# Attention: three of a key tile's four maximum products placed behind the value products

## What is computed

```python
# x: (2, 2048, 256); H = 256, NH = 16 heads, D = 16
hn = _layernorm(x, ln1_g, ln1_b)
q = (hn @ wq + bq).reshape(b, s, NH, D).transpose(0, 2, 1, 3)
k = (hn @ wk + bk).reshape(b, s, NH, D).transpose(0, 2, 1, 3)
v = (hn @ wv + bv).reshape(b, s, NH, D).transpose(0, 2, 1, 3)
scores = jnp.einsum('bhqd,bhkd->bhqk', q, k) / jnp.sqrt(jnp.float32(D))
attn = jax.nn.softmax(scores, axis=-1)
o = jnp.einsum('bhqk,bhkd->bhqd', attn, v)
```

## Time and profile before

| | |
|---|---|
| median of 3 runs | 3656.47 us (3653.67 to 3663.54) |
| the profiled execution | 3660.14 us, its span 3658.3 us |
| attention, first S to last exponential | 1521.1 to 2948 us of the span |
| VectorE's reductions (line 694) | 2048, 1269.9 us busy |
| TensorE's X, S, V | 2048, 2048 and 4096 matmul records |

### The profile page before, as it was taken

The page is one execution under the profiler, slowest core; times in us unless marked ns, Lnnn a source line. Parts: engine busy times, 40 slices in busy tenths (PEclk is TensorE's granted clock), DMA queues, the critical chain, the costliest instruction groups (busy, mean ns, idle before and its releaser), DMA issues. The chain is left out here.

```text
span 3658.3 us, 43277 instructions
## 1 busy us (share of the span) xinstructions
PE 3051.2 (83%) x12860; PEld 1452.0 (40%) x12860; DVE 2599.6 (71%) x3622; ACT 1732.7 (47%) x2113; POOL 816.1 (22%) x397
## 2 busy tenths in 40 slices
PE   5768788798797775999999999999999957769994
PEld 3333234243343332433333333333333324658883
DVE  5527989889889896998989898989899539101111
ACT  2225554554554541276767676767677820101110
POOL 2204555455455465000000000000000015220003
PEclk9879899899898887599999999999999965579997
DMA  4532121111121114644444444444444044044554
GB/s 150 162 114 87 64 74 71 64 64 67 60 75 67 54 71 64 119 63 63 62 63 62 63 62 63 62 63 62 63 62 62 10 115 124 18 148 163 171 170 129
DMA packets 230405, 306.67 MB, mean 84 GB/s; under 512 B 111467, under 2 KB 179332, under 8 KB 215748
## 3 DMA queue, kind: packets, MB, share of 16 engines
q1 hardware_dynamic: 225988, 291.60, 35.0%
q0 software_dynamic: 4224, 12.59, 1.2%
HBM read 240.38 MB, written 63.21 MB: 83 GB/s over the span
## 5 line engine op out<-in xcount | busy, mean ns | idle before, releaser
L694 DVE TENSOR_REDUCE attn_mx<-attn_pX 128x1 f32<-128x512 f32 x2048 | 1269.9, 682 | 153.8 <-PE attn_pX L608 153.7
L674 ACT ACTIVATE attn_pr<-attn_pS 128x1024 f32<-128x1024 f32 x1024 | 991.8, 1021 | 514.8 <-PE attn_pS L621 513.5
L608 PE MATMUL attn_pX<-attn_ks,attn_qs 48*128 48x512 f32 x2048 | 767.3, 500 | 79.2 <-DMA attn_vs<-v_d 25.1
L1142 PE MATMUL mamba_pY<-mamba_g,mamba_ident 128*128 128x512 f32 x1024 | 527.9, 665 | 212.0 <-DVE mamba_g L1266 211.9
L1253 DVE TENSOR_TENSOR_SCAN mamba_h<-mamba_pA,mamba_hs,mamba_db 128x512 f32<-128x512 f32 x512 | 617.6, 1263 | 98.4 <-ACT mamba_pA L996 92.8
L608 PEld LDWEIGHTS attn_pX<-attn_ks,attn_qs 48*128 48x128 f32 x2048 | 312.3, 193 | 792.4 <-DVE attn_mx L694 717.4
L937 POOL TENSOR_TENSOR mamba_db<-mamba_bq,mamba_u 128x2048 f32<-128x2048 f32 x128 | 577.8, 4514 | 72.0 <-DVE mamba_u L1213 71.7
L996 ACT ACTIVATE mamba_pA<-mamba_dt,mamba_an 128x512 f32<-128x512 f32 x512 | 351.7, 691 | 452.7 <-DVE mamba_h L1253 452.5
L631 PE MATMUL attn_pO<-attn_pr,attn_vs 128*17 128x512 f32 x4096 | 554.2, 614 | 0.8 <-ACT attn_pr L674 0.7
L621 PE MATMUL attn_pS<-attn_qs,attn_ks 50*128 50x512 f32 x2048 | 467.6, 414 | 23.7 <-issue 19.0
L1142 PEld LDWEIGHTS mamba_pY<-mamba_g,mamba_ident 128*128 128x128 f32 x1024 | 211.7, 213 | 513.7 <-DVE mamba_g L1266 269.7
(11 more groups left out here) (170 smaller groups left out, 2036.3 us busy)
## 6 DMA issues: line engine op xcount, KB each, us to landing
mamba_bq<-bc_d SPq DMA_DIRECT2D x64, 1024.0 KB, 4.7
attn_ks<-parts_d SPq DMA_DIRECT2D x192, 256.0 KB, 9.1
exp_w<-in_w SPq DMA_DIRECT2D x46, 1024.0 KB, 4.9
attn_vs<-v_d SPq DMA_DIRECT2D x32, 544.0 KB, 15.8
parts_d<-proj_qp SPq DMA_DIRECT2D x32, 512.0 KB, 3.0
attn_qs<-parts_d SPq DMA_DIRECT2D x192, 64.0 KB, 8.3
attn_qs<-attn_mt SPq DMA_DIRECT2D x512, 1.0 KB
oraw_d<-attn_oe SPq DMA_DIRECT2D x32, 256.0 KB, 2.1
```

Of the source, the lines that this page charges most:

```text
L608: pe.matmul(pX[bank(s, n)][:, :], QS[slot][rows, pair, qt * P:(qt + 1) * P], KS[slot][rows, pair, part * BANK:(part + 1) * BANK], start=Tr ...
L674: act.activation(PR[2 * (kt % 2) + pair][:, :, :], pS[pair][:, :, :], ACT.Exp, scale=HD ** -0.5).then_inc(p_sb, 1)
L694: dve.tensor_reduce(MX[:, col:col + 1], pX[bank(s, n)][:, :], AX.X, ALU.max).then_inc(x_max, 1)
L1142: mm = pe.matmul(pY[j][:, :], ident[:, :], G[k % 2][:, n, :], start=False, stop=(q == NQ - 1 and n == QN - 1))
```

## The change

Only TensorE's order in `body` changes. Before, two X stand ahead of V and two behind; now X0 alone stands ahead and X1, X2, X3 behind it. The products, their banks, their semaphores and every other engine's order are as they were.

```diff
-                        for pair in range(2):
-                            if ahead:
-                                scores(*ahead[0], pair)
-                            if left >= 2:
-                                scores_max(i, s + 2, n + pair * SM_KT // 4, n + (pair + 1) * SM_KT // 4)
+                        if ahead:
+                            scores(*ahead[0], 0)
+                        if left >= 2:
+                            scores_max(i, s + 2, n, n + 1)
+                        if ahead:
+                            scores(*ahead[0], 1)
                         values(i, s, kt)
                         if left >= 2:
-                            scores_max(i, s + 2, n + SM_KT // 2, n + SM_KT)
+                            scores_max(i, s + 2, n + 1, n + SM_KT)
```

## The result

The changed kernel takes 3791.74 us (median of 4 runs, 3785.57 to 3837.65) against 3660.01 us before (4 runs, 3653.67 to 3666.77), 3.6% longer by the medians; the ratio of the means is 1.039, interval 1.033 to 1.044. The forecast was 3770 us, range 3700 to 3809. The profiled execution has a span of 3793.9 us, 135.6 us more than before.

What follows compares the result with a forecast made beforehand. The prediction took a closed TensorE-VectorE loop through the X banks, 2.70 us a tile, as the bound. Adding 104 us (steady tiles), 3 (ring restarts) and 6 (half clock), 113 in all, to 3656.5 gave 3770 us, range 3700 to 3809.

Steps and rivals of the forecast that it cites:

- The loop of five terms: Steady attention tile, X1's reduction round to its next: 0.69 + 0.06 + 0.67 + 0.98 + 0.54 = 2.94 us, against 2.70.
- From X0 to V, 0.67 us: With pair S1 unhidden between them, V starts 0.67 us after X0 (0.52 to 0.76), against 0.43 behind X1 before.
- Behind V: X1 follows V by 0.98 us, its reduction starts 0.54 us later; a third X there costs nothing.
- The idle time of VectorE: Sign: about 0.44 us once a tile before X1's reduction; before line 694 rising from 153.7 to some 255 us.
- 432 tiles times 0.24, 104 us: Steady tiles: each of 432 takes 0.24 us more, 104 us in all (39 to 143).
- Item boundaries: Periods there stay at 3.3 us; only eight places where the bank ring restarts cost up to 0.5 us each, 3 us.
- Half clock, 6 us: Behind loop jumps, unhidden S1 adds 0.4 us to each of 12 to 20 half-clock periods: 6 us (0 to 9).
- The range: 8 in 10 range for the total: 3700 us (39 and some 4 us added) to 3809 us (143 and 9).
- The rival of the clock: More waiting drops the granted clock to half inside items: 4.54 us a period, 795 us more, 4450 us; chance 3%.
- S1 hidden beside X0: No-change rival: S1 runs wholly beside X0, V follows by 0.43 to 0.45 us, total 3657 to 3668 us; chance 4%.
- TensorE's own length: Faster rival: X1, X2, X3, S0, S0, X0 pack the array without a gap, total 3536 to 3557 us; chance 4%.

Runs made afterwards that it cites:

- g1: Changed kernel's order with S1 moved ahead of X0 and V cut into two column halves in 14 of 16 tiles; 3672.49 us, 0.995 of the kernel before.
- h1: g1 with the X banks in an order that closes on itself after four items; 3665.41 us, 0.9975 of the kernel before.

## Why the prediction was right, point by point

- *The loop of five terms.* Right. It gave the steady tile of six orders of the products, and of the one with two banks, to within 0.02 us.
- *From X0 to V, 0.67 us.* It measured 0.65 us. The value came from two rows that held its parts; the upper end, from a row with one matmul more, would have been 0.1 too high.
- *Behind V.* Right: X1's reduction starts 0.53 us after X1, and a third X costs nothing. The idle time of VectorE was to be 0.44 us a tile and is 0.44; over the whole it rose to 294 us, not 255, mostly because of the tiles at half clock.
- *432 tiles times 0.24, 104 us.* Right: the 408 tiles that stayed steady cost 96.8 us, 0.237 each, which makes 102.5 for all 432.
- *Item boundaries.* Right: 3.28 us before and after. Where the ring starts anew it is 4.13 us instead of 3.62, the 0.5 us that were named. There are seven such places and not eight: X is done for items 4, 8 and so on to 28 there.
- *Half clock, 6 us.* This term was mis-sized. It counted only a dearer pair in the tiles that were at half clock already. In fact 22 tiles more fell to it or stayed in it; they cost 33.8 us, 5.2 of which the first term had already counted. This is where most of the 22 us between forecast and result come from, as the runs' mean granted clocks show too.
- *The range.* That 3791.74 us lies inside it is in part luck. Its upper end, 3809 us, was made of the 0.76 us from X0 to V that did not occur; no room had been left for falls of the clock in new places, and that room served for them.
- *The rival of the clock* was given 3% as a fall throughout the items. It came in small: not in the steady tiles, which kept 1.00 as forecast, but behind the one idle stretch of 1.5 us in a turn.
- *S1 hidden beside X0*: no; it ends 0.73 us after X0's start (2102.82 to 2102.91 + 0.64), and V follows X0 by 0.65 us. *TensorE's own length*: the packing of three X and S0 is there (X3 and S0's first matmul both start at 2101.87), and was worth nothing, since TensorE waited anyway.

## What to carry to other kernels

When two engines each wait for the other once a tile, write down the loop that closes through the buffer and add up its links: the product that waits for the buffer, all that stands between it and the long block, the block, and the first product behind it. Work that is free while it stands ahead of the waiting product costs what it holds the long block back by when it stands behind it: here 0.24 us a tile for one pair, some 100 us in all. Before counting on a shorter loop, see how the engine's clock takes the new pattern: with V split the tile was 0.2 us shorter in its rows, and almost none of that reached the total. Each run's mean granted clock tells the two apart: plot the time against it before you call a change worthless.

## What had not been expected of the hardware

- An idle stretch of TensorE of 1.51 us was followed by the half clock in five of seven turns; one of 1.14 us in the kernel before in none of seven. With V split it fell behind one of 1.12 us (g1), and in h1 eight times behind 0.79 us or less. The length of the idle stretch alone does not decide it.
- How long the clock then stays at half differs between executions and places of the same loop: 10 to 17 us with the kernel before, 3 to 96 us with S1 in the loop, 3 to 68 us with V split, while TensorE's matmul rows fill nearly all of the time.
- The two column halves of V take 0.56 us each against 0.98 us for the whole, so that cutting V costs about 0.14 us.
